# Counting edges by target bucket: the fourth one-hot of each group made by ScalarE as relu(1 - |bucket - i|)

## The reference

```python
edge_index = jnp.stack([src, dst])
h = jnp.maximum(_layernorm(x, axis=-1), 0.0)
x = x + L0(h, edge_index, edge_type_4, ...)        # message MLP per edge type, summed by dst, GRU
x = x + L1(relu(layernorm(x)), edge_index, ...)    # softmax attention over the edges grouped by src
x = x + L2(relu(layernorm(x)), ..., edge_type_64)  # relational convolution, summed by dst
x = x + L3(relu(layernorm(x)), edge_index, ...)    # three graph convolutions, summed by dst
```

## Time and profile before

| what | us |
|---|---|
| median of three runs | 9144.29 |
| the three runs | 9132.01, 9144.29, 9151.67 |
| the profiled execution, its own time | 9128.77 |
| its span, first to last instruction | 9126.7 |
| POOL busy | 6422.1 (70%) |
| PE busy | 5175.1 (57%) |
| DVE busy | 5003.5 (55%) |
| ACT busy | 2412.3 (26%) |

### The profile page before, as it was taken

The page is one execution under the profiler, slowest core; times in us unless marked ns, Lnnn a source line. Parts: engine busy times, 40 slices in busy tenths (PEclk is TensorE's granted clock), DMA queues, the critical chain, the costliest instruction groups (busy, mean ns, idle before and its releaser), DMA issues. The chain is left out here.

```text
span 9126.7 us, 131725 instructions
## 1 busy us (share of the span) xinstructions
PE 5175.1 (57%) x32947; PEld 4359.8 (48%) x32947; DVE 5003.5 (55%) x16106; ACT 2412.3 (26%) x7474; POOL 6422.1 (70%) x6585
## 2 busy tenths in 40 slices
PE   6657447888780015566589999544444444444443
PEld 4326337788440014454379999533333333333332
DVE  9988635566853016666668888633333333333333
ACT  0001024444020016666468888300000000000000
POOL 2777777777778777777357777477776777767776
PEclk9878779999585558877799999755555555555555
DMA  1001012223100002222399999322223222221223
GB/s 39 3 6 37 28 47 55 55 55 51 19 15 18 1 18 53 53 53 53 86 349 386 379 383 386 130 53 52 52 52 57 53 52 52 51 58 52 53 52 58
DMA packets 392742, 799.66 MB, mean 88 GB/s; under 512 B 165514, under 2 KB 202188, under 8 KB 392012
## 3 DMA queue, kind: packets, MB, share of 16 engines
q0 software_dynamic: 302976, 715.02, 27.2%
q1 hardware_dynamic: 89100, 79.83, 2.8%
q10 hardware_dynamic: 320, 0.80, 0.0%
HBM read 729.24 MB, written 65.95 MB: 87 GB/s over the span
## 5 line engine op out<-in xcount | busy, mean ns | idle before, releaser
L171 POOL DMA_INDIRECT edge_rows<-tab,all_slots x3328 | 3209.4, 964 | 1448.6 <-issue 971.4
L1978 PE MATMUL edge_psum<-edge_rows,edge_onehot 128*128 128x128 f32 x4992 | 1290.5, 440 | 1913.4 <-DMA edge_rows<-tab,all_slots 1741.3
L1978 PEld LDWEIGHTS edge_psum<-edge_rows,edge_onehot 128*128 128x128 f32 x4992 | 1110.9, 327 | 2092.7 <-issue 1932.3
L1967 DVE TENSOR_TENSOR acc_acc<-acc_acc,edge_psum 128x128 f32 x2496 | 716.1, 287 | 2055.2 <-PE edge_psum L1978 1787.1
L1769 PE MATMUL edge_p_m<-edge_rows,edge_onehot 128*128 128x128 f32 x9984 | 1128.6, 276 | 44.5 <-ACT edge_rows L1701 40.4
L1769 PEld LDWEIGHTS edge_p_m<-edge_rows,edge_onehot 128*128 128x128 f32 x9984 | 1121.0, 192 | 52.1 <-issue 32.9
L507 POOL DMA_INDIRECT slots_d<-all_slots,pro_row_d x782 | 784.7, 1003 | 401.1 <-issue 246.3
L1701 ACT ACTIVATE edge_rows<-edge_rows,edge_coef 128x128 f32<-128x128 f32 x3328 | 995.4, 387 | 171.4 <-DMA edge_rows<-tab,all_slots 171.4
L171 POOL DMA_INDIRECT edge_rows<-tab,edge_slots x832 | 812.3, 976 | 269.7 <-issue 253.3
L1068 POOL DMA_INDIRECT slots_s<-acc_pays,acc_row_s x782 | 805.8, 1030 | 275.9 <-issue 246.3
L888 POOL DMA_INDIRECT all_x<-tab_src,all_slots x832 | 788.6, 948 | 267.9 <-issue 253.4
(11 more groups left out here) (366 smaller groups left out, 8655.3 us busy)
## 6 DMA issues: line engine op xcount, KB each, us to landing
edge_rows<-tab,all_slots POOLq DMA_INDIRECT x3328, 2.5
tab<-tab_o SPq DMA_DIRECT2D x50, 512.0 KB, 2.6
all_x<-tab_src,all_slots POOLq DMA_INDIRECT x832
edge_rows<-tab,edge_slots POOLq DMA_INDIRECT x832, 2.5
tab_src<-all_x SPq DMA_DIRECT2D x50, 260.0 KB, 2.0
slots_d<-all_slots,pro_row_d POOLq DMA_INDIRECT x782
slots_s<-acc_pays,acc_row_s POOLq DMA_INDIRECT x782, 2.1
tab<-acc_acc SPq DMA_DIRECT2D x18, 512.0 KB, 3.2
```

The source lines that it names most:

```text
L171: pool.indirect_dma_start(out=rows[:, slot, j, :], out_offset=None, in_=table[:, :], in_offset=bass.IndirectOffsetOnAxis(ap=index, axis=0) ...
L1967: v.tensor_tensor(at, at, psum[:, slot % 2, j * P:(j + 1) * P], ALU.add).then_inc(q["added"], 1)
L1978: m = pe.matmul(psum[:, slot % 2, j * P:(j + 1) * P], onehot[:, slot % 2, j, :], rows[:, slot, j, :], start=True, stop=True)
```

## The change

For every group of four columns in the counting (not in the ranking) VectorE makes three one-hots, and ScalarE the fourth. ScalarE has no comparison; it makes |bucket - i| (L276 of the changed kernel) into one of two buffers, waits on its own semaphore `distant` for it, and then relu(1 - |bucket - i|) (L279) into the ring, which is 1 where i is the bucket and 0 elsewhere. The buffers lie in `negoff`, a tile that is free at that time. TensorE waits for both semaphores. ScalarE waits for `bucketed`, a new semaphore that VectorE gives when the bucket numbers are there.

```diff
--- before.py
+++ after.py
@@ -245,6 +245,8 @@
         self.own = place(2 * COLS * n).rearrange("p (z c) -> p z c", z=2) if together else None
         self.hot, self.used, self.counted, self.totalled, self.firsts, self.based, self.pieced, self.ranked, self.owned, self.picked = (
             s.sem(f"{name}_{x}") for x in ("hot", "used", "counted", "totalled", "firsts", "based", "pieced", "ranked", "owned", "picked"))
+        self.apart = None if together else K["negoff"][:, 0:n].bitcast(BF16).rearrange("p (z n) -> p z n", z=2)
+        self.distant, self.hot_too = s.sem(f"{name}_distant"), s.sem(f"{name}_hot_too")
 
     def columns(self, k):
         return range(COLS * k, min(COLS * (k + 1), EC))
@@ -261,12 +263,25 @@
             v.tensor_tensor(self.hot_of(i, 0, n).rearrange("p (c b) -> p c b", b=self.n), bcast_mid(self.K["iota"][:, 0:self.n], n),
                             bcast_last(self.bucket[:, c0:c0 + n], self.n), ALU.is_equal).then_inc(self.hot, 1)
         else:
-            for j, c in enumerate(columns):
+            for j, c in enumerate(columns[0:COLS - 1] if i < KG else columns):
                 o = v.tensor_scalar(self.hot_of(i, j), self.K["iota_b"][:, 0:self.n], self.bucket[:, c:c + 1], None, ALU.is_equal)
             o.then_inc(self.hot, 1)
 
+    def hots_too(self, act, k):
+
+        columns = self.columns(k)
+        if len(columns) == COLS:
+            c = columns[-1]
+            wait(act, self.hot_too, k - 1)
+            act.activation(self.apart[:, k % 2, :], self.K["iota_b"][:, 0:self.n], ACT.Abs, scale=-1.0, bias=self.bucket[:, c:c + 1]).then_inc(self.distant, 1)
+            act.wait_ge(self.distant, k + 1)
+            wait(act, self.used, k - 3)
+            act.activation(self.hot_of(k, COLS - 1), self.apart[:, k % 2, :], ACT.Relu, scale=-1.0, bias=self.K["ones"][:, 0:1]).then_inc(self.hot_too, 1)
+
     def count(self, pe, k):
         pe.wait_ge(self.hot, k + 1)
+        if not self.together and len(self.columns(k)) == COLS:
+            pe.wait_ge(self.hot_too, k + 1)
         h, q, n = k // QH, k % QH, len(self.columns(k))
         row = self.K["slide"][:, QH - 1 - q:2 * QH - 1 - q]
         for j in range(n):
@@ -406,7 +421,7 @@
         piece = s.sb("piece", [P, 3])
         bank = s.ps("bank", [P, 8, 512])
         names = ("memset", "iota", "made", "cleared", "loaded_d", "loaded_r", "patterned", "zeroed", "keys", "paid", "paid_s", "rows_d", "rows_s",
-                 "dve", "pool", "cols", "passed", "table", "tabled", "ends", "x_cleared", "x_loaded", "centred", "squared", "normed",
+                 "dve", "pool", "bucketed", "cols", "passed", "table", "tabled", "ends", "x_cleared", "x_loaded", "centred", "squared", "normed",
                  "w_cleared", "w_loaded", "turned", "copied", "pa_done", "pb_done", "pa_out", "pb_out", "triangles", "slots_in")
         q = {n: s.sem(n) for n in names}
         stored_a = [s.sem(f"stored_a{z}") for z in range(2)]
@@ -519,6 +534,9 @@
             act.wait_ge(q["keys"], 1)
             act.activation(payd[:, :, F_KEY], keyi, ACT.Copy).then_inc(q["paid"], 1)
             act.activation(pays[:, :, 0].bitcast(I32), dst, ACT.Copy)
+            act.wait_ge(q["bucketed"], 1)
+            for k in range(KG):
+                D_.hots_too(act, k)
             act.wait_ge(q["keys"], 2)
             act.activation(pays[:, :, 1], keyi_s, ACT.Copy).then_inc(q["paid_s"], 1)
 
@@ -578,6 +596,7 @@
             link(v.tensor_scalar(keyi, dst, P - 1, None, ALU.bitwise_and))
             v.nop().then_inc(q["keys"], 1)
             link(v.scalar_tensor_tensor(bucket_d, wini, float(TYPES), typ, ALU.mult, ALU.add))
+            v.nop().then_inc(q["bucketed"], 1)
             for k in range(KG):
                 D_.hots(v, k)
             D_.take_counts(v)
```

## The result

The changed kernel takes 9170.11 us (median of 8 runs, 9163.16 to 9176.3), the kernel before 9145.63 (8 runs, 9132.01 to 9151.67). The ratio is 1.0029, with a 95% interval of 1.0018 to 1.0040: slower by 24.5 us of the medians, where 26 were predicted. One run of the kernel before among those beside the experiments took 11076 us, over a fifth more than all others, and is left out of the ratios.

What follows compares the result with a forecast made beforehand. The chain of counting ahead of the first scatter was taken to bound the prologue; ScalarE's 0.835 us a group over 195 groups, started late, moves the copy from 155.62 to 181.93, so 9144.29 + 26 = 9170, range 9149 to 9190.

Steps and rivals of the forecast that it cites:

- The bound: Prologue: counting sets the first scatter, which sets the end; a shift of the first scatter shifts everything behind it equally.
- The pace: ScalarE in the counting: distance 447, wait 36, next distance 352 ns later, so 835 ns a group against VectorE's 726.
- The choice of 36 against 107 ns: ScalarE's relu waiting for its own distance: 36 ns taken from `edges0`, 107 from `edges1` kept for the range.
- Rival A: ScalarE's wait costs 107 ns as in `edges1`: pace 906 ns, shift 40 us, time 9184; 11 in 100.
- VectorE's gap: Counting: VectorE, making three one-hots, was to be idle some 0.29 us in each group.
- The late start: ScalarE's first distance, behind L521, starts at 18.15, 4.9 us after VectorE's first one-hot.
- What was cost at nothing: TensorE's second wait and rate, the `nop` for `bucketed`, buffers and ring add nothing; 2 us allowed for TensorE's clock.
- TensorE's rate: Counting: 24 matmuls in 4.18 us even before its clock rose, 0.70 a group, under 0.835, so cost at nothing.
- A profile's span of 9153: Whole program: predicted span of the profile after; the profiled execution before took 9128.77, 15.5 below its median.
- B: Rival: ScalarE's wait is hidden, pace 0.704, counting ends about 156.5, time 9145, no change; 8 in 100.
- C: Rival: VectorE's three one-hots decide, counting ends 35 us earlier, time 9109; 5 in 100.
- D: Rival: ScalarE takes at least three times VectorE's time per instruction, shift 76 us, time 9220; 1 in 100.

Runs made afterwards that it cites:

- both make it: Changed kernel with VectorE making all four one-hots again, ScalarE's pairs going to an unread spare buffer TensorE still waits for; ratio 1.0036 to the kernel before.
- the experiment without the wait: Changed kernel with four distance buffers instead of two and the next group's distance ahead of this one's relu; ratio 1.0001 to the kernel before.
- Pairs first: Changed kernel with ScalarE's pairs put ahead of its five copies of the payloads; ratio 1.0024 to the kernel before.
- third pass: Changed kernel with a third ScalarE instruction per group, a second distance into an unread spare buffer; ratio 1.0078 to the kernel before.
- three of four: Changed kernel with ScalarE serving three groups in four, four buffers, next distance ahead of the relu, pairs ahead of copies; ratio 0.9971 to the kernel before.

## Why the prediction was right

**The bound.** That the first scatter sets the end of the prologue, and the counting the first scatter, held: over ten profiles the copy of the counts moves between 129.3 and 225.3, the first scatter follows it by 22.2 to 23.2, and the ratios follow in the same order, but for the changed kernel and "both make it", whose copies come 0.1 us apart and whose intervals overlap. VectorE's idle time before `edges0` stays long (152.90 us after, 148.45 before).

**The pace.** 0.835 was worked out, 0.845 measured. The distance lasts 445 ns (447 expected) and the relu starts some 30 ns behind it (36; 6.3 us over 195 in the rows below), but the relu lasts 461 and the next distance starts 0.37 behind it instead of 0.352. That is the one term of the pace that was mis-sized: 194 x 0.0105 = 2.0 us, and with it the copy of the counts came at 184.1 instead of 181.9. ScalarE's groups in the first 600 us (count, busy and mean ns, idle before):

```profile
L279 ACT ACTIVATE acc_acc<-pair_negoff,all_ones 128x200 bf16<-128x200 bf16 x195 | 89.9, 461 | 6.3
L276 ACT ACTIVATE pair_negoff<-all_iota_b,acc_acc 128x200 bf16<-128x200 bf16 x195 | 86.8, 445 | 0.0
```

The Trainium skill (ScalarE: Activation LUTs, "What ACT_TABLE_LOAD costs") gives 280 ns + 0.833 ns a column with a pointer as bias, an estimate of 447 ns for 200 columns. The trace agrees for the distance (445) and, in the experiment without the wait, for both (447); the relu that waits lasts 14 ns more.

**The choice of 36 against 107 ns** for the wait was right: 30 measured. Rival A's price is thereby out, and with it the idea that the row of `edges1` shows the wait itself; what the register work there costs wasn't tried.

**VectorE's gap.** 0.29 us idle in each group were expected and 0.21 came. The expectation took 3 x 0.1815 off the pace, but the last of three one-hots isn't overlapped by a next one, so three are busy for 0.64. It costs nothing, as the pace is ScalarE's.

**The late start.** 4.9 us were expected, 5.0 are what the pairs ahead of the copies bring.

**What was cost at nothing** held, to 1 us. From the copy of the counts to the first scatter it is 23.2 us instead of 22.2, within the 2 us allowed. TensorE's mean granted clock (third figure from the end) is lower there, 0.63 after against 0.70 before:

```profile
155.00:178.00 23.00, 14.50 (x64) 7.40 (x63) 18.89 (x89) 0.00 (x0) 0.22 (x1) 0.70 0.00 0
```

```profile
184.00:207.00 23.00, 15.31 (x59) 7.81 (x58) 18.24 (x85) 0.00 (x0) 0.00 (x0) 0.63 0.00 1
```

The clock alone doesn't explain it, and the cause stays open. "Pairs first" has 0.63 and 23.2 us as well, but the third pass has the full clock over its whole stretch and still takes 22.9, and the kernel before takes 22.2 in one profile and 22.6 in the other at about 0.70. The third pass, from its copy of the counts to its first scatter:

```profile
225.34:248.26 22.92, 14.91 (x58) 7.74 (x58) 18.46 (x86) 0.00 (x0) 0.00 (x0) 1.00 0.00 0
```

TensorE's rate was read from a row that doesn't show it: 24 matmuls in 4.18 us fit VectorE's pace (5 x 0.726 + 0.55), and the granted clock of those first us is given as 1.00, so no row shows one that has yet to rise. The term is settled by "three of four" instead, where TensorE does a group in 0.59 us and is busy for 46 of 50.

**Median and profile.** 28.5 us to the copy, 1.0 to the first scatter and 5.1 in the scatters make the 34.6 us of the two spans. The 5.1 us can't be laid to the change: the unchanged kernel shows 6.1 between its own two profiles, and over all ten the stretch follows no order of the edits (the third pass, slowest of all, has the shortest). A profile's span of 9153 was predicted and 9161.3 came; the median of 9170 was met to 0.1 us, which is luck beyond the few us that the sum can claim. By the trace the change itself costs 28.5 to 29.5 us, and the ratio's interval, 16 to 37 us, holds both that and the 24.5 of the medians.

**Which rivals had a point.** B and C named their own conditions, a pace of 0.70 and VectorE's three deciding. The change has neither, so this is no merit of theirs in the forecast; two of the experiments supply them, one by four buffers, the other by a smaller share, and the times came where the rivals had put them or on the way there (C's 35 us are out of reach while ScalarE takes three groups of four; 27 came). D, three times VectorE's time for each instruction, has nothing for it: 0.352 between starts against 0.1815 is 1.9 times.

## What to carry to other kernels

Work that is moved to an idle engine counts there with its own latency: two dependent instructions cost a whole duration plus a start (0.845 us here), not two starts (0.702), until the next item's first is put between them. Compare pace with pace before sharing: here 0.845 on the new engine against 0.726 on the old one that it was to relieve, and the partners meet at every group, so the slower decides. Then give the new engine the share that its pace allows, and start it when the other starts.

## What the runs showed of the hardware

The same ScalarE instruction on 128x200 lasts 445 to 447 ns, 461 when it had waited for the one before it, and 477 where three stand in a row for a group. Those that needn't wait for the one just ahead start 0.351 to 0.352 us apart, whether they last 447 or 477. Here the duration in a trace is no measure of what one more instruction costs; the distance between starts is. The 782 scatters, for which POOL waits for another engine only once, took 1029.9 to 1036.1 us over ten profiles, and the preparations ahead of the first one-hot ended at 11.7 in three of them and at 13.2 to 13.4 in the other seven, in no order of the edits: a difference of 6 us between two single profiles of this kernel says nothing.
